# Expert choice by marking maxima in place, and gates spread as two float32r parts

## The reference

```python
scores = softmax(xf @ gw + gb)                        # T x 32
scores_g = scores.reshape(T, 8, 4)                    # 8 groups of 4 experts
group_scores = sum(top_k(scores_g, 2))                # the two best of each group
keep = the 4 groups of highest group_scores
masked = where(keep, scores_g, -inf)
indices = top_k(masked, 4)                            # 4 experts
cw = zeros(T, 32) with the scores of these 4 experts
for e in range(32):
    h = silu(xf @ w1[e] + b1[e]) * (xf @ w3[e] + b3[e])
    y += cw[:, e] * (h @ w2[e] + b2[e])
z = silu(xf @ sw1 + sb1) * (xf @ sw3 + sb3) @ sw2 + sb2    # shared expert
x = x + y + z
```

## Time and profile before

| | us |
|---|---|
| median of three runs | 1479.75 |
| lowest and highest run | 1478.83, 1482.98 |
| the profiled execution, its own time | 1484.09 |
| its span in the trace | 1482.3 |
| mean granted clock of TensorE, share of full | 0.948 |

### The profile page before, as it was taken

The page is one execution under the profiler, slowest core; times in us unless marked ns, Lnnn a source line. Parts: engine busy times, 40 slices in busy tenths (PEclk is TensorE's granted clock), DMA queues, the critical chain, the costliest instruction groups (busy, mean ns, idle before and its releaser), DMA issues.

```text
span 1482.3 us, 20178 instructions
## 1 busy us (share of the span) xinstructions
PE 1401.2 (95%) x6191; PEld 793.7 (54%) x6191; DVE 1106.2 (75%) x1494; ACT 806.8 (54%) x1625; POOL 936.7 (63%) x540
## 2 busy tenths in 40 slices
PE   5999998876999999999999999999999999998798
PEld 3877775522555554555554555455555555555465
DVE  8976666279779688778868878887796886675755
ACT  4668886330556555555655655555565555454232
POOL 3001113231688888988988897898888899885010
PEclk9999999655899999999999999999999999997799
DMA  6640000030000200020020020002002000000011
GB/s 161 201 137 17 18 17 7 17 75 0 0 1 1 49 1 1 6 44 1 1 48 1 1 45 5 0 2 48 1 1 45 1 1 0 2 0 13 18 37 39
DMA packets 77370, 39.41 MB, mean 27 GB/s; under 512 B 62047, under 2 KB 70000, under 8 KB 77002
## 3 DMA queue, kind: packets, MB, share of 16 engines
q1 hardware_dynamic: 77290, 38.36, 10.4%
HBM read 24.66 MB, written 13.68 MB: 26 GB/s over the span
## 4 chain that ended last, share of the span: by engine, by line
PE 86%; DVE 8%; DMA 2%; ACT 2%; issue 1%; POOL 0%; SPq 0%; ACTq 0%; DVEq 0%; POOLq 0%
PE ps L1394 25%; PE ps L1381 14%; PE ps L1382 12%; PE ps L1347 9%; DVE chunk_max L948 3%; PE ps L1334 3%; DMA v_scratch<-v_stage 2%; PE ps L1537 2%; PE ps L1209 2%; PE ps L1207 2%; PE ps L1218 2%; PE ps L1208 2%; PE ps L1219 2%; PE ps L1220 2%; PE ps L1326 1%
## 5 line engine op out<-in xcount | busy, mean ns | idle before, releaser
L521 POOL TENSOR_TENSOR psums<-psums,probs 126x1024 f32<-126x1024 f32 (+1 forms) x392 | 821.8, 2096 | 122.7 <-ACT probs L714 75.4
L714 ACT ACTIVATE probs<-ps 126x512 f32<-126x512 f32 (+1 forms) x816 | 416.4, 617 | 273.4 <-PE ps L1382 261.3
L948 DVE TENSOR_REDUCE chunk_max<-ps 128x2 f32<-128x1008 f32 (+1 forms) x416 | 472.5, 1181 | 76.5 <-PE ps L1347 75.0
L1394 PE MATMUL ps<-probs,v_mem 126*64 126x512 f32 (+1 forms) x1632 | 389.6, 598 | 0.0
L1381 PE MATMUL ps<-q_heads,ring 128*126 128x512 f32 (+1 forms) x816 | 343.3, 421 | 1.0
L1382 PE MATMUL ps<-q_low,ring 128*126 128x512 f32 (+1 forms) x816 | 322.7, 395 | 0.0
L999 DVE TENSOR_TENSOR xn<-xn,probs 126x512 f32<-126x512 f32 x126 | 231.6, 1838 | 29.9 <-ACT probs L714 25.7
L680 ACT CAST ring<-ps 64x252 fp32r<-64x252 f32 (+1 forms) x356 | 128.3, 360 | 136.1 <-PE ps L1334 133.0
L1394 PEld LDWEIGHTS ps<-probs,v_mem 126*64 126x64 f32 (+1 forms) x1632 | 111.5, 136 | 165.5 <-issue 121.2
L1381 PEld LDWEIGHTS ps<-q_heads,ring 128*126 128x126 f32 (+1 forms) x816 | 152.1, 186 | 88.5 <-issue 44.7
L1347 PE MATMUL ps<-ring,q_heads 64*128 64x504 f32 (+1 forms) x416 | 173.7, 483 | 21.0 <-DVE chunk_max L948 12.7
(11 more groups left out here) (205 smaller groups left out, 1444.6 us busy)
## 6 DMA issues: line engine op xcount, KB each, us to landing
v_scratch<-v_stage SPq DMA_DIRECT2D x51, 252.0 KB
v_mem<-v_scratch SPq DMA_DIRECT2D x8, 1606.5 KB
ctx_mem<-in_ctx_t SPq DMA_DIRECT2D x3, 803.2 KB, 8.7
vslot<-in_ctx_rows SPq DMA_DIRECT2D x51, 47.2 KB
pair_w<-in_f_pairs SPq DMA_DIRECT2D x17, 128.0 KB, 2.1
pair_w<-in_f_pairs SPq DMA_DIRECT2D x17, 65.0 KB, 1.8
x_tok<-in_x SPq DMA_DIRECT2D x1, 512.0 KB, 4.3
wo<-in_c_wo SPq DMA_DIRECT2D x1, 512.0 KB
```

The source lines that it names most:

```text
L521: pool.tensor_tensor(sums[0:r, 0:width], sums[0:r, 0:width], probs[0:r, n % PROBS, 0:width], ALU.add).then_inc(c_sum, 1)
L714: act.activation(probs[0:r, n % PROBS, cols(half)], ps[0:r, score_bank(t, half), :], ACT.Exp, scale=float(HD) ** -0.5).then_inc(c_exped, 1)
L948: dve.tensor_reduce(chunk_max[:, h % 2, i:i + 2, c], ps[:, banks[0]:banks[1] + 1, 0:group_tiles(c) * KT], AX, ALU.max).then_inc(c_reduced, 1)
L1394: ins = pe.matmul(ps[half * HD:(half + 1) * HD, B_ACC, :], v_tiles[0:r, h % 2, t, :], probs[0:r, n % PROBS, cols(half)], start=(t == 0), s ...
```

## The change

It has four parts.

1. `first_four` no longer looks for indices. After the eight largest values are found, places 4 to 7 of `top8` are overwritten with -9 (which no candidate equals), and a matching replacement copies the candidates with each of the four values turned into the mark 9. The cast, the compare and the sum are gone. The mask arithmetic behind the first call is recast for marks, and the multiply behind the second compares with the mark and multiplies in one instruction.
2. The gates are spread from two float32r parts on 64 partitions. ScalarE copies the transposed `cw` from PSUM to the high part, VectorE subtracts that from PSUM to make the low part, and only then ScalarE makes the plain `cw_t`. The transposes go to PSUM banks 1 and 3. `spread1` is loaded as bfloat16 of 64 rows and copied to float32r by ScalarE ahead of the exponential.
3. The first gate matmul comes before the two `b2` matmuls, which wait for `cw_t`.
4. TensorE's loop over pairs is written out in full, so `spread1` is addressed by constants.

```diff
@@ loads and ScalarE
-                             (sb2[:, :], f1_sb2), (spread1[:, :, :], spread1_in)):
+                             (sb2[:, :], f1_sb2), (spread_raw[:, :, :], spread1_in[0:2 * E1])):
+            act.wait_ge(in_f1, 16 * 5)
+            act.copy(spread1[:, :, :], spread_raw[:, :, :])
             act.wait_ge(g_exp, 1)
@@
             act.wait_ge(g_cwt, 1)
-            act.copy(halves(cw_t), ps[0:E1, 4:6, :]).then_inc(g_cwtsb, 1)
+            act.copy(halves(cw_parts[0:E1, :]), ps[0:E1, 1:4:2, :]).then_inc(g_cwtsb, 1)
+            act.wait_ge(g_spread_ready, 1)
+            act.copy(halves(cw_t), ps[0:E1, 1:4:2, :]).then_inc(g_cwtsb, 1)
@@ VectorE, first_four
                 link(ins)
+                link(dve.memset(top8[:, :, TOPK:8], UNUSED))
                 for t in range(TT):
-                    ins = dve.max_index(idx8[:, t, :], top8[:, t, :], values[:, t, :])
+                    ins = dve.match_replace(marked[:, t, :], top8[:, t, :], values[:, t, :], MARK)
                 link(ins)
-                link(dve.tensor_copy(idxf8[:, :, :], idx8[:, :, :]))
-                hits = ranks[:, 0:TT * TOPK * width].rearrange("p (t r e) -> p t r e", t=TT, r=TOPK)
-                link(dve.tensor_tensor(hits, iota[:, 0:width].unsqueeze(1).unsqueeze(1).to_broadcast([P, TT, TOPK, width]),
-                                       idxf8[:, :, 0:TOPK].unsqueeze(3).to_broadcast([P, TT, TOPK, width]), ALU.is_equal))
-                link(dve.tensor_reduce(chosen, hits.rearrange("p t r e -> p t e r"), AX, ALU.add))
@@ VectorE, masks and parts
-            link(dve.tensor_scalar(keep, keep, 2.0, -2.0, ALU.mult, ALU.add))
+            link(dve.tensor_scalar(keep, keep, MARK, 2.0, ALU.not_equal, ALU.mult))
-                                   over(keep, TT, GROUPS, E1 // GROUPS), ALU.add))
+                                   over(keep, TT, GROUPS, E1 // GROUPS), ALU.subtract))
             first_four(gp, E1, cw)
-            dve.tensor_tensor(cw, cw, gl, ALU.mult).then_inc(g_cw, 1)
+            dve.scalar_tensor_tensor(out=cw, in0=cw, scalar=MARK, in1=gl, op0=ALU.is_equal, op1=ALU.mult).then_inc(g_cw, 1)
             dve.wait_ge(g_cwtsb, 1)
-            link(dve.tensor_copy(cw_3[0:E1, :], cw_t))
-            link(dve.tensor_tensor(cw_r, cw_t, cw_3[0:E1, :], ALU.subtract))
-            link(dve.tensor_copy(cw_b[:, :], cw_r))
-            link(dve.tensor_copy(cw_3[E1:2 * E1, :], cw_b[:, :]))
-            link(dve.tensor_tensor(cw_r, cw_r, cw_b[:, :], ALU.subtract))
-            dve.tensor_copy(cw_3[2 * E1:3 * E1, :], cw_r).then_inc(g_spread_ready, 1)
+            dve.tensor_tensor(halves(cw_parts[E1:2 * E1, :]), ps[0:E1, 1:4:2, :], halves(f32(cw_parts[0:E1, :])),
+                              ALU.subtract).then_inc(g_spread_ready, 1)
@@ TensorE
-                pe.wait_ge(g_hg[half], pair)
-                pe.matmul(ps[:, 4 + half, :], spread1[:, bass.ds(pair, 1), :].rearrange("p a c -> p (a c)"),
-                          cw_3[:, cols(half)], start=True, stop=True).then_inc(g_gate[half], 1)
+                if pair:
+                    pe.wait_ge(g_hg[half], pair)
+                pe.matmul(ps[:, 4 + half, :], spread1[:, pair, :],
+                          cw_parts[:, cols(half)], start=True, stop=True).then_inc(g_gate[half], 1)
@@
-            pe.wait_ge(g_cwtsb, 1)
+            pe.wait_ge(g_spread_ready, 1)
+            gate(0, 0)
+            pe.wait_ge(g_cwtsb, 2)
             for half in range(2):
                 pe.matmul(ps[:, 6 + half, :], b2_1[:, :], cw_t[:, cols(half)], start=False, stop=False, skip_group_check=True)
-            pe.wait_ge(g_spread_ready, 1)
-            gate(0, 0)
@@
-            with pe.Fori(0, G1 // 2 - 1) as i:
-                two_pairs(i, False)
-            two_pairs(G1 // 2 - 1, True)
+            for i in range(G1 // 2):
+                two_pairs(i, i == G1 // 2 - 1)
```

More of the change, by code:

```diff
@@ L38 @@
 PAIR_W = 3 * P + 2
+MARK, UNUSED = 9.0, -9.0
 BANKS_S = 5
@@ L254, in build_program @@
         pmax, pmin, qmax, qmin, keep = (over_ctx(TT, GROUPS) for _ in range(5))
-        cw_t, cw_r = over_ctx(TOK)[0:E1, :], over_ctx(TOK)[0:E1, :]
-        x3_t, ranks = over_ctx(TOK), over_ctx(TT * TOPK * E1)
+        cw_t = over_ctx(TOK)[0:E1, :]
+        x3_t = over_ctx(TOK)
         pair_w = sb("pair_w", [P, 2, PAIR_W])
@@ L317, in build_program @@
             parts = sb_c("parts", [P, 2 * TOK + 8 * P], F32R)
-            cw_b = sb_c("cw_b", [E1, TOK], BF16)
-            cw_3 = sb_c("cw_3", [3 * E1, TOK], BF16)
+            cw_parts = sb_c("cw_parts", [2 * E1, TOK], F32R)
+            spread1 = sb_c("spread1", [2 * E1, G1, P], F32R)
             silu = sb_c("silu", [P, 2, HALF])
             hgate = sb_c("hgate", [P, 2, HALF])
+            spread_raw = sb_c("spread_raw", [2 * E1, G1, P], BF16)
             gw = sb_c("gw", [P, E1])
@@ L325, in build_program @@
             sb2 = sb_c("sb2", [P, 1])
-            spread1 = sb_c("spread1", [3 * E1, G1, P], BF16)
         x_hi, x_lo = parts[:, 0:TOK], parts[:, TOK:2 * TOK]
@@ L1083, in _, with first_four @@
             link(dve.tensor_tensor(pmax, pmax, pmin, ALU.add))
-            def first_four(values, width, chosen):
+            def first_four(values, width, marked):
                 for t in range(TT):
@@ L1550, in _ @@
             for t in range(TT):
-                ins = pe.transpose(ps[0:E1, 4 + t // 4, tile_cols(t % 4)], cw[:, t, :], ident[:, :])
+                ins = pe.transpose(ps[0:E1, 1 + 2 * (t // 4), tile_cols(t % 4)], cw[:, t, :], ident[:, :])
             ins.then_inc(g_cwt, 1)
-            pe.wait_ge(g_cwtsb, 1)
+            pe.wait_ge(g_spread_ready, 1)
+            gate(0, 0)
+            pe.wait_ge(g_cwtsb, 2)
             for half in range(2):
                 pe.matmul(ps[:, 6 + half, :], b2_1[:, :], cw_t[:, cols(half)], start=False, stop=False, skip_group_check=True)
-            pe.wait_ge(g_spread_ready, 1)
-            gate(0, 0)
             def two_pairs(i, last):
-                m1, m2 = pe.snap(2 * i + 1), pe.snap(2 * i + 2)
-                m3 = pe.snap(2 * i + 3)
+                m1, m2, m3 = 2 * i + 1, 2 * i + 2, 2 * i + 3
                 up(m1, 1, 1, m2)
@@ L1571, in two_pairs @@
                 if not last:
-                    up(m3, 1, 0, pe.snap(2 * i + 4))
+                    up(m3, 1, 0, 2 * i + 4)
                     gate(m2, 0)
                 down(0, 1, g_hg, m2, stop=last)
-            with pe.Fori(0, G1 // 2 - 1) as i:
-                two_pairs(i, False)
-            two_pairs(G1 // 2 - 1, True)
+            for i in range(G1 // 2):
+                two_pairs(i, i == G1 // 2 - 1)
 def kernel(**inputs):
```

## The result

The changed kernel is slower, by half a percent. Its median is 1487.12 us (1484.94 to 1489.48, six runs) against 1479.42 for the kernel before (1475.94 to 1482.98, six runs). The ratio is 1.0052, with an interval of 1.0035 to 1.0069. The forecast was 1475.1 in a range up to 1479.5, so the time lies outside it, on the other side.

What follows compares the result with a forecast made beforehand. The prediction took a serial VectorE chain to bound the stage before the expert loop, and TensorE the loop. Terms 4.44 - 0.75 + 0.0 + 0.9 = 4.6 us gave 1479.75 - 4.6 = 1475.1, range 1470.5 to 1479.5.

Steps and rivals of the forecast that it cites:

- The loop: Expert loop: 32 gate matmuls from 96 bfloat16 to 64 float32r rows, and unrolling, priced at zero; 3 to 6 us without cover.
- Rival C: Expert loop: gate weights not loaded under the matmul ahead, 0.19 open 31 times, 5.9 us; 1481.0 in all; 7%.
- gating of the shared expert earlier: VectorE, first search: cast, compare and sum go (1.47 us), a memset comes (0.23); gating starts 1.24 us earlier.
- weights ready earlier: VectorE, both searches together: 1.24 + 3.20 = 4.44 us earlier, 1384.12 in place of 1388.56.
- taken back by TensorE's down and up group: Before the transposes: TensorE's down and up matmuls end at 1384.87, later than the weights, so 0.75 us is lost.
- transposes earlier: TensorE's transposes of the weights start 3.7 us earlier, after the loss to the down and up matmuls.
- copy to first up matmul: Making the gate parts: 6.78 us against 6.76, b2 uncovered at half clock; gain taken as 0.0, 1.7 at full clock.
- clock behind it: Behind the first up matmul: full clock returns sooner as TensorE is dense from b2 on; 0.9 us gained, bounds nothing to 2.6.
- The silu: ScalarE ends the silu at 1378.10, before the earlier gating at 1379.14, so the gating need not wait for it.
- the copy of spread1: ScalarE's new copy ahead of the exponential: 1.9 to 2.1 us, covered, priced zero; 0.4 if it took 3 us.
- Rival D: Replacement costs 1.4 us more, ScalarE's copy 0.4, and down and up run at half clock: 0.7 gained, 1479.0; 5%.
- rivals A and B: A: down and up at half clock, no clock gain, 1477.2, 22%. B: full clock through transposes, b2, loop, 1471.0, 21%.

Runs made afterwards that it cites:

- the trace of 65 rows: The kernel with 96 rows, its gate cut to 65 rows (one row of zeros in place of 32): 1475.29 us, 0.9969 of the kernel before.
- the kernel with 96 rows: The changed kernel with its gate matmul on 96 rows in place of 64, 32 of them zeros: 1475.79 us, 0.997 of the kernel before.
- the fastest kernel: The kernel with 96 rows, plain copy first, float32r parts made from it by VectorE, b2 matmuls ahead of the first gate: 1471.22 us, 0.9946.

## Why the prediction was wrong

**The step that failed is "The loop".** I priced the gate's change from 96 to 64 rows "at nothing: the cover is the preceding matmul". It costs 0.39 us each time, 12 us in all, and the cover is what it takes away. I read the price of the gate off the up matmuls beside it, which are float32r but use all 128 rows, and off the gate itself, which used 96. The type was looked at, the row count wasn't. Rival C had the right place and the right sign ("weights of the gate aren't loaded under the matmul ahead"), and at 5.9 us half the size: it put one load in the open, 0.19, where three gaps grew, by 0.10 at the gate, 0.20 at down and 0.10 behind it; how these divide between open loads and anything else isn't shown. I gave it 7% since "float32r loads of 0.19 lie hidden in every up group". That was true and didn't bear on the matter. The idle time of 0.27 ahead of the gate's load, which I took as its sign, was no sign: in the kernel before it costs nothing (the gate pitch is 0.23).

**The row that would have told was in the trace of the kernel before.** The attention part has matmuls on 64 rows between ones on 128 (timeline of TensorE):

```profile
1187.58 0.39 PE L1381 MATMUL ps<-q_heads,ring 128*126 128x512 f32 x1
1187.81 0.40 PE L1382 MATMUL ps<-q_low,ring 128*126 128x512 f32 x1
1188.14 0.50 PE L1347 MATMUL ps<-ring,q_heads 64*128 64x504 f32 x1
1188.14 0.73 PE L1347 MATMUL ps<-ring,q_low 64*128 64x504 f32 x2
1188.48 0.39 PE L1347 MATMUL ps<-ring,q_heads 64*128 64x504 f32 x1
1188.80 0.65 PE L1394 MATMUL ps<-probs,v_mem 126*64 126x512 f32 x2
```

From 128 rows to 128 rows it is 0.23, from 128 to 64 it is 0.33, and between the two 64-row steps 0.34. (A step is two matmuls here, `q_heads` and `q_low`, that start at the same time.) The same 0.50 that the changed kernel's gate shows as its duration stands there too. I had taken my bounds from the stage at hand, which has no matmul on 64 rows.

**The rest of the sum held, in part by luck.** In order of time, from the same fixed instruction:

| step | forecast | the two traces |
|---|---|---|
| gating of the shared expert earlier | 1.24 | 1.31 |
| weights ready earlier | 4.44 | 4.59 |
| taken back by TensorE's down and up group | 0.75 | 0.96 |
| transposes earlier | 3.7 | 3.63 |
| the transposes themselves | 0 | 0.88 |
| copy to first up matmul | 0.0 | 0.86 |
| clock behind it | 0.9 | -0.1 |
| **loop** | **0** | **-12.1** |
| sum | 4.6 | -6.8 |

The sum takes the rows from "transposes earlier" on, since the three above it make that one; counted from the layer norm to the end the traces differ by -6.6. The first four are the marks: replacing costs what searching did, and TensorE takes 1 us back since it became the last. The transposes and the copy-to-up path gained because TensorE's clock was full for a longer part of them (b2 took 2.56 us, not 3.43); I had put that gain into the clock term, behind the up matmul, where there was none: the clock was at half for 5.5 us behind it, and 5.25 before. Together the three clock-bound terms gave 1.6 where 0.9 was forecast. The forecast of 0.0 for copy to up matmul stood for a stretch at half clock, and there it was too kind: it put the b2 pieces at 3.43 us, where the earlier trace rows already had 3.78, and with all of them at half clock, in the trace of 65 rows, the path took 7.11 us and not 6.78, 0.35 more than before. That these terms come near the forecast is luck of the executions: kernels with one and the same order ahead of the loop differ between the layer norm and the end by 2.2 us (115.7 with 96 rows, 117.9 with 65) and by 1.5 (121.0 in the kernel before, 119.5 with its loop written out), while the loss in the loop is 12. That the uncovered b2 matmuls eat the gain of the shorter split was right. Against the median of its runs, the kernel with 96 rows gained 4.3 us, where my sum without the crossings said 4.6. That is the edge of 0.3% that I had named.

The silu, the copy of spread1 and the unrolling cost nothing, as forecast. Rival D was wrong in both terms of its own (dearer replacement, dearer copy), rivals A and B in that they took the loop for granted.

## What to carry to other kernels

When a matmul's shape is changed, look up what its neighbours on TensorE have for a shape, above all the number of rows, and price the pair. Cutting a small matmul to 64 rows inside a dense full-array stream cost 0.28 to 0.39 us each time here and saved nothing, and a single row of zeros beyond 64 took that cost away. And when a serial chain on a slow engine is shortened, check what ran under it: here matmuls of 2 to 4 us, by the clock, lost their cover, and putting them back under it took 2.4 us off this path in the traces.

## What the hardware showed that I had not expected

- A 64-row gate between 128-row matmuls costs 0.39 us over a 96-row one with float32r weights, and 0.28 with bfloat16 ones, at full clock; at 65 rows it costs nothing. The load of the first 64-row matmul's weights starts together with it (1398.65) and not under the one ahead, and so does that of the 128-row matmul behind it (1399.08).
- A second 64-row matmul right behind the first adds 0.22 us, so the price is per crossing, as far as two in a row show it.
- A replacing match (value load and replacement) takes as long as the index search: eight pairs took 1.21 us at width 8 and 1.41 at width 32, the search 1.22 and 1.42. The weights came 4.59 us earlier, where 4.44 was reckoned at equal price.
- The granted clock fell in the midst of b2 matmuls on 32 rows in the changed kernel, though TensorE was busy then, and stayed full in the one trace of the fastest kernel, where they began 1.1 us behind the transposes. Where it falls and rises moves by some 2 us between executions of the same order, and the time in front of the loop with it (30.57 and 32.85 us with 96 and 65 rows).
